# Skip term as a GpSimd product and an identity matmul, a bias in 16-bit rows, new instruction lists

## The reference

```python
x = x + attn(cond(x, k, k, w, u, time_emb), ...)      # scan, then a chunked state-space layer
x = x + ffn(cond2(x, k, k, w2, u2, time_emb), ...)    # scan, then a ternary feed-forward net

# cond: forward and backward scans of ek and ek*v along the tokens, a and b decayed each step
base = sigmoid(r) * (num / maximum(den, 1e-08))

# attn: z, x, B, C, dt = u @ in_proj_w; x = silu(causal_conv1d(x)); y = decayed scores times v
y = y + D_param[None, :, None, None] * v              # the skip term
y = y * rsqrt(mean(y * y) + RMS_EPS) * norm_scale * silu(z)
return y @ out_proj_w

# ffn: rms_norm, 8-bit rounding per row, ternary weights with one scale
h = silu(einsum(xq, w1q) + b1)                        # the first bias
h = layer_norm(gelu(h), ln_g, ln_b)
return einsum(hq, w2q) + b2
```

## Time and profile before

| | |
|---|---|
| three runs, median (lowest to highest) | 205.26 us (204.13 to 205.44) |
| profiled execution, span from first to last instruction | 201.1 us; no other time is given for it |
| VectorE busy | 178.6 us (89%), 320 instructions |
| ScalarE busy | 159.8 us (79%), 293 instructions |
| TensorE busy | 159.6 us (79%), 903 instructions |
| GpSimd busy | 100.3 us (50%), 172 instructions |
| DMA | 11.55 MB, mean 57 GB/s |

### The profile page before, as it was taken

The page is one execution under the profiler, slowest core; times in us unless marked ns, Lnnn a source line. Parts: engine busy times, 40 slices in busy tenths (PEclk is TensorE's granted clock), DMA queues, the critical chain, the costliest instruction groups (busy, mean ns, idle before and its releaser), DMA issues.

```text
span 201.1 us, 3190 instructions
## 1 busy us (share of the span) xinstructions
PE 159.6 (79%) x903; PEld 117.4 (58%) x908; DVE 178.6 (89%) x320; ACT 159.8 (79%) x293; POOL 100.3 (50%) x172
## 2 busy tenths in 40 slices
PE   7800039459799999999999999999999999672844
PEld 5600038334589867698757488957668766350633
DVE  2899999999999999899999899979866769998991
ACT  5860599969699279998789999899999886877632
POOL 3609759000426523758700086467455287858570
PEclk9975557958999999999999999999999999999699
DMA  4999603200000000000000000000240000602312
GB/s 133 320 385 382 248 2 104 106 3 2 1 0 3 0 0 2 4 3 0 2 2 3 0 0 3 0 2 0 54 96 14 0 0 0 130 7 49 81 60 96
DMA packets 12304, 11.55 MB, mean 57 GB/s; under 512 B 7680, under 2 KB 10368, under 8 KB 12032
## 3 DMA queue, kind: packets, MB, share of 16 engines
q1 hardware_dynamic: 11856, 11.33, 18.1%
q10 hardware_dynamic: 432, 0.03, 0.1%
HBM read 8.69 MB, written 1.05 MB: 48 GB/s over the span
## 4 chain that ended last, share of the span: by engine, by line
PE 45%; DVE 14%; ACT 12%; issue 12%; POOL 8%; DMA 5%; SPq 3%; POOLq 1%; DVEq 0%; ACTq 0%
PE banks L1688 41%; DVE Ys L1239 5%; DMA wn<-wn 4%; PE banks L1685 3%; DVE Fs L1230 3%; DVE nd L1250 3%; SPq L355 2%; ACT Ys L744 1%; POOL qr L514 1%; ACT Ys L742 1%; POOL wn L576 1%; ACT dec L691 1%; ACT dec L844 1%; ACT D L724 1%; DMA cum_t<-cum_s 1%
## 5 line engine op out<-in xcount | busy, mean ns | idle before, releaser
L1688 PE MATMUL banks<-inw,uT 128*128 128x8 f32 (+1 forms) x64 | 21.7, 465 | 19.4 <-DVE uT L1277 19.4
L1688 PEld LDWEIGHTS banks<-inw,uT 128*128 128x128 f32 x64 | 10.9, 217 | 24.7 <-issue 24.5
L1230 DVE TENSOR_TENSOR_SCAN Fs<-D,E 128x514 f32<-128x514 f32 x16 | 23.0, 1460 | 0.5 <-POOL D L449 0.5
L1688 PE MATMUL banks<-uT,inw 128*128 128x256 f32 x80 | 20.3, 398 | 0.0
L1239 DVE TENSOR_TENSOR_SCAN Ys<-D,Fs 128x514 f32<-128x514 f32 x16 | 19.7, 1250 | 0.0
L1323 DVE SCALAR_TENSOR_TENSOR cv<-banks,cols,cv 128x255 f32<-128x255 f32 (+2 forms) x48 | 19.4, 472 | 0.1
L1688 PEld LDWEIGHTS banks<-uT,inw 128*128 128x128 f32 x80 | 15.2, 197 | 4.2 <-issue 2.1
L508 POOL TENSOR_TENSOR vs<-vv,grow 128x512 f32<-128x512 f32 x4 | 4.5, 1121 | 25.8 <-issue 20.3
L1688 PEld LDWEIGHTS banks<-vv,skips 128*128 128x128 f32 x128 | 15.2, 192 | 1.9 <-issue 1.8
L495 POOL TENSOR_TENSOR own<-own,vT 128x1024 f32<-128x1024 f32 x4 | 12.1, 3025 | 8.4 <-DVE own L1220 8.4
L1688 PE MATMUL banks<-vv,dec 128*128 128x64 f32 x128 | 15.6, 275 | 0.0
(11 more groups left out here) (205 smaller groups left out, 469.4 us busy)
## 6 DMA issues: line engine op xcount, KB each, us to landing
wn<-in_w_dram SPq DMA_DIRECT2D x2, 1024.0 KB, 11.1
inw<-in_in_w_dram SPq DMA_DIRECT2D x1, 1160.0 KB, 10.8
vT<-in_kT_dram SPq DMA_DIRECT2D x4, 256.0 KB, 8.2
xcT<-in_xT_dram SPq DMA_DIRECT2D x4, 256.0 KB, 9.6
...
```

The lines of the kernel that those rows point to most:

```text
L1230: dve.tensor_tensor_scan(Fs[:, w, k], D[:, w, 0:CT * TS], E[:, b % 2, k].rearrange("p c t -> p (c t)"), 0.0, ALU.mult, ALU.add).then_inc(f ...
L1688: return pe.matmul(dst, lhsT, rhs, start=start, stop=stop)
```

## The change

Four things change together.

The skip term. GpSimd multiplies a tile's vv by D, head by head, into skv (`skip_values`, one instruction of 128x512), and `within` adds it by one matmul with the identity in place of eight small ones. `make_skips` is gone from ScalarE.

The first bias. b1 is loaded to 67 rows and split into three bf16 pieces, held in rows 0 to 31, 32 to 63 and 64 to 66 (`bias_piece` on ScalarE and `bias_rest` on GpSimd, once). The factor 1/al1 of each row is split into three pieces on GpSimd (`bias_factors`), turned by TensorE (`factor_turns`) and copied by ScalarE (`factor_rows`). The bias is then a bf16 matmul in which nine rows hold the products of pieces and the rest are zero. `ffn_diag` and its diagonal are gone.

Scales of tiles. al1 and al2 are computed on GpSimd instead of VectorE, the reciprocal of al1 is gone, and buffers of one column per tile replace those of one column per half, which drops some waits.

All call lists, the order of the loads and the banks of `HOME` are new. Ten groups of dummy matmuls become six.

```diff
 def within(b, c):
-    pe.wait_ge(cumi_ok, 2)
+    pe.wait_ge(ident_ok, 2)
+    pe.wait_ge(sk_ok, TT * b + c + 1)
+    mm(bank, ident[:], skv[:, c], True, False)
     pe.wait_ge(vv_ok, TT * b + c + 1)
-    for h in range(NH):
-        part = slice(h * HD, (h + 1) * HD)
-        mm(bank[:, part], skips[:, h], vv[:, b % 2, c, part], h == 0, False)
     pe.wait_ge(att_ok, TT * b + c + 1)
...
+def skip_values(b, c):
+    pool.wait_ge(heads_in, 16)
+    pool.wait_ge(vv_ok, TT * b + c + 1)
+    if b >= 1:
+        pool.wait_ge(y_ps, TT * (b - 1) + c + 1)
+    pool.tensor_tensor(by_head(skv[:, c]), by_head(vv[:, b % 2, c]),
+                       heads[:, 2, :].unsqueeze(2).broadcast_to([P, NH, HD]), ALU.mult).then_inc(sk_ok, 1)
...
-def ffn_diag(i):
-    pool.tensor_scalar(diag[:, i % 2], ident[:], ral1[:, i:i + 1], ..., ALU.mult, ALU.mult).then_inc(dg_ok, 1)
+def bias_rest(k):
+    n = 64 - 32 * k
+    pool.wait_ge(b1_ok, 2 * k + 1)
+    pool.tensor_tensor(b1f[0:n], b1f[0:n], b1r[0:n], ALU.subtract).then_inc(b1_ok, 1)
+def bias_factors(p):
+    s = tiles_of(p)
+    pool.wait_ge(hr_ok, 2 * p + 2)
+    pool.wait_ge(hq_ok, p + 1)
+    pool.wait_ge(wmean_ok, 3)
+    for i in range(s.start, s.stop):
+        pool.tensor_scalar(fac[:, i:i + 1], hmv[:, i:i + 1], hr[:, i:i + 1], wrec[:, 0:1], ALU.mult, ALU.mult)
+        last = pool.tensor_scalar(al1[:, i:i + 1], hm[:, i:i + 1], hr[:, i:i + 1],
+                                  (wmean if i < FIRST_TANH else whalf)[:, 0:1], ALU.mult, ALU.mult)
+    last.then_inc(al1_ok, 1)
+    pool.wait_ge(al1_ok, p + 1)
+    for k in range(3):
...
+            pool.tensor_tensor(fact[:, s], fac[:, s], hq[:, s], ALU.mult).then_inc(fac_ok, 1)
...
+        pool.tensor_scalar(fpc[:, s, :, k], fact[:, s].unsqueeze(2).broadcast_to([P, s.stop - s.start, 3]),
+                           1.0, 0.0, ALU.mult, ALU.add).then_inc(fac_ok, 1)
...
+def bias_piece(k):
+    n = (KB, 64, 32)[k]
+    act.activation(b1r[0:n], b1f[0:n], ACT.Copy).then_inc(b1_ok, 1)
+def factor_rows(p):
+    act.wait_ge(fT_ps, p + 1)
+    act.activation(fT[:, s.start * P:s.stop * P], at("factor_turns", p)[0:KB, ...], ACT.Copy).then_inc(fT_ok, 1)
...
 def ffn_up(i):
-    pe.wait_ge(dg_ok, i + 1)
+    pe.wait_ge(fT_ok, part_of(i) + 1)
+    pe.wait_ge(b1_ok, 5)
     for g in range(2):
-        last = mm(ffn_mid(i)[:, half], diag[:, i % 2], b1b[:, half], False, True)
+        last = mm(ffn_mid(i)[:, half], fT[:, i * P:(i + 1) * P], b1r[:, half], False, True)
...
-def ffn_in_back(p):
-def ffn_back(i):
+    pool.tensor_scalar(al2[:, s], qm[:, s], gq[:, s], wmean[:, 1:2], ALU.mult, ALU.mult).then_inc(al2_ok, 1)
```

More of the change, by code:

```diff
@@ L1126, in _ @@
             ffn_square(5)
+            factor_rows(4)
             ffn_gelu(6)
@@ L1549, in _ @@
             ratio(2)
+            gated(2)
+            clip_weights(0)
+            forward(3, 0, 0)
             residual(0)
-            wkv_min(3)
-            gated(2)
+            attend(1, 0)
+            softplus_in(2)
+            own_min(3)
             ffn_in(0)
-            attend(1, 0)
-            ffn_in_max(0)
-            forward(3, 0, 0)
-            forward(3, 0, 1)
-            y_scale(1)
-            attend(1, 1)
-            softplus_in(2)
-            ffn_in_scale(0)
-            ffn_in_back(0)
@@ L1563, in _ @@
             features(2)
-            clip_weights(0)
-            own_min(3)
             softplus_out(2)
             conv_taps(2, 1)
+            running_sums(2)
+            ffn_in_max(0)
+            attend(1, 1)
+            ffn_in_scale(0)
             norm_gate(1, 0)
+            make_less16()
+            y_scale(1)
+            conv_taps(2, 0)
+            forward(3, 0, 1)
             norm_gate(1, 1)
-            running_sums(2)
+            forward(3, 1, 0)
+            forward(3, 1, 1)
@@ L1585, in _ @@
+            ffn_in(1)
             ratio(3)
-            attend(2, 1)
-            gated(3)
-            ffn_in(1)
             y_scale(2)
             ffn_in_max(1)
-            clip_weights(1)
+            gated(3)
+            ffn_mean(1)
             ffn_center(0)
             ffn_shift(0)
+            ffn_in_scale(1)
+            ffn_max(0)
+            softplus_in(3)
             norm_gate(2, 0)
-            ffn_mean(1)
-            ffn_in_scale(1)
+            features(3)
+            softplus_out(3)
@@ L1597, in _ @@
             norm_gate(2, 1)
-            ffn_max(0)
+            conv_taps(3, 1)
+            conv_taps(3, 0)
+            running_sums(3)
             ffn_center(1)
             ffn_shift(1)
-            softplus_in(3)
-            ffn_in_back(1)
-            softplus_out(3)
-            features(3)
-            conv_taps(3, 1)
             ffn_scale(0)
             ffn_max(1)
-            conv_taps(3, 0)
-            running_sums(3)
+            residual(2)
             ffn_mean(2)
+            y_scale(3)
@@ L1814, in project, with factor_turns @@
                 last.then_inc(o_ps, 1)
+            def factor_turns(p):
+                s = tiles_of(p)
+                pe.wait_ge(masks_ok, 4)
+                pe.wait_ge(fac_ok, 6 * p + 7)
+                for k, i in enumerate(range(s.start, s.stop)):
+                    last = mm(at("factor_turns", p)[0:KB, k * P:(k + 1) * P],
+                              fpc[:, i].rearrange("p j k -> p (j k)")[:, 0:KB], identb[:], True, True)
+                last.then_inc(fT_ps, 1)
             def q1_turns(p):
```

931 lines of the change are left out of this document (469 added, 462 removed).

## The result

The changed kernel takes 223.4 us (median of four runs) against 204.7 us for the kernel before on the same chip. The ratio here is 1.081 (95% interval 1.072 to 1.090): 8% slower, outside the range.

The account below looks back on a forecast made before the run. VectorE was taken to set the pace to about 145 us, then TensorE and ScalarE, then a dependent tail. 201.1 - 4.7 + 2.0 + 0.5 + 2.5 - 4.0 = 197.4, plus 4.2 gives 201.6 us; range 195 to 209.

Parts of the forecast that it names:

- TensorE and the sizes of its work: Skip and bias matmuls: net 12 to 15 us less TensorE work, none counted up to 145 us because VectorE covers it.
- The start, +0.5: First forward scan waits behind the second k load, starting at 9.8 us; uT(0) ends 0.5 us later (0 to +2.7).
- VectorE, -4.7: ffn_back, ffn_in_back and its reciprocals leave VectorE, saving 4.7 us, two thirds in the tail or just before it.
- GpSimd against VectorE, +2.0: GpSimd's 13.5 us of new products delay VectorE at a rate of 0.15, costing 2.0 us (bounds 0 and 13.5).
- rival A: Ports decide: GpSimd's products cost VectorE 9 us, mostly between 40 and 110 us; time 212.6 us; chance 0.15.
- its check (over 182): VectorE's busy total over 182 us, instead of 174 to 177, would show that the ports rival holds.
- the cover for bias_factors: GpSimd's factor work hides if al1 and al2 precede ffn_silu and ffn_out; otherwise 2.6 us between ffn_in_scale and ffn_up.
- The new order, the middle (+2.5): Batch 1's features on ScalarE reached at about 69 us, VectorE ready at about 67; costs 2.5 us (0 to 5).
- from 142 us on (-4.0): In the tail, earlier TensorE, one table load fewer and ffn_max filling gaps save 4.0 us (0 to 8).
- The sentence on what would make it wrong: Prediction fails if an unwalked list entry, a late load or a bank's wait on TensorE, stalls several engines at once.

Follow-up runs that it names:

- Lists alone: Changed kernel with skip term and first bias as before, keeping the new lists, banks, load order and GpSimd scales: 223.8 us, 1.095 against the kernel before.
- the trace with 80 rows: Changed kernel with the first bias loaded to 80 partitions instead of 67: 219.2 us, ratio 1.070 to the kernel before.
- the only repair that helped: Changed kernel with 80 rows, the front of pass 0 reordered on VectorE and TensorE, then GpSimd and ScalarE: 215.8 us, 1.058 against the kernel before.

## Why the prediction was wrong

**TensorE and the sizes of its work: right.** 146.0 us for "about 145", skip products 8.2 for 8.6, bias 5.2 and turns 1.4 for 9.1. So was the care to count none of it; that a cut of it could be worth less than nothing, by the clock and by lost cover, was not in the bounds. The run without the skip products is that case, 3 us.

**The start, +0.5: right where it looked.** The first scan began at 9.20 us (9.8 said), uT(0) ended at 29.0 (28.9). It counted bytes and not rows, so the load of 67 rows is missing: 2.0 points in the kernel before, 1.1 in the changed one, there not clear of noise.

**VectorE, -4.7: the instructions went, the time did not.** The al2 part alone is worth nothing in the kernel before.

**GpSimd against VectorE, +2.0: mis-sized.** VectorE's busy time says 8.8: 182.7 against 178.6 - 4.7. That is rival A's 9, and its check (over 182) came true. Its sign did not: none of the 16 forward scans took over 1.23 us; it was dtp (4.32), the backward scans (up to 2.23) and small ones that stood. GpSimd's own busy time was mis-sized with it, 144.0 us for about 125. And the cover for bias_factors was gone, by 12.5 us and not by 2.6: its small instructions took up to 3.38 us each beside VectorE's scans. But rival A isn't the cause. Lists alone lose 9.5% with GpSimd busy 116.5 us, and it gave 212.6 us at its worst.

**The new order, the middle (+2.5) and from 142 us on (-4.0): the steps that failed.** I walked ScalarE to features(1) at one place and took the rest of pass 0 as unchanged; residual(0) is 15.9 us late in the changed kernel and 14.7 in the lists alone. What the walk missed in the lists: softplus_out(0) behind wkv_min(2), twelve conv taps (4.8 us) ahead of running_sums(0), TensorE's gates behind it, and ScalarE's first decays behind a seed and four table loads. In the lists alone these decays start at 65.5 us instead of 52.3. From residual(2) to the last output the kernel before takes 56.3 us and the changed one 57.2: +0.9 for my -4.0. The sentence on what would make it wrong, an entry not walked that stalls several engines, named it with no price and no chance.

**Shown:** that the lists (with the banks, the order of the loads and the scales) carry the loss; that 67 rows cost 2.0% in the kernel before; that the skip part gains 2.5 points in the new lists with the old bias and costs 3 in the old lists; that a front delay isn't recovered in the old lists. **Argued only:** which of the calls ahead of residual(0) cost how much. In the trace with 80 rows VectorE is busy 86.1 us up to it instead of 76.4, of which 4.3 are calls that stood behind it before (wkv_min(3), gated(2), clip_weights(0), forward(3,0,0)) and the rest stretched ones, but the run that moved them gained nothing. The traces name TensorE's own order instead (its log decays and gate_in(0,1) behind the conv turns, at a granted clock of 0.66), and that stays a reading of traces too. **Open:** what each part of the lists is worth, since the only repair that helped took 1.070 to 1.058; and whether the skip part costs over 3% in the old lists by GpSimd's products (VectorE busy 4.8 us longer) or by TensorE's identity products (8.6 us).
